# Fourth layer's attention: natural scores ahead of the next queries, and values and gate products ahead of the turned maxima

## The reference, cut to what matters

```python
x = x + tanh(g_xattn[3]) * L3_xattn(layernorm(x), ctx, Wq, bq, Wk, bk, Wv, bv, Wp, bp)
# L3_xattn, 16 heads of 8 features:
q = (x @ Wq.T + bq).reshape(Bx, Nx, H, D)
k = (ctx @ Wk.T + bk).reshape(Bx, -1, H, D)
v = (ctx @ Wv.T + bv).reshape(Bx, -1, H, D)
att = softmax(einsum('bnhd,bthd->bhnt', q, k) / sqrt(D))
y = einsum('bhnt,bthd->bnhd', att, v).reshape(Bx, Nx, C) @ Wp.T + bp
# followed by x = x + tanh(g_ffn[3]) * L3_ffn(layernorm(x), ...), a mixture of 8 experts, 2 per token
```

## Time and profile before

| what | us |
|---|---|
| median of 3 runs | 1149.16 (1143.81 to 1149.33) |
| span of the profiled execution, first to last instruction | 1134.3 |
| median less that span | 14.9 |
| a pass of the fourth layer's attention, plain (pass 10) | 9.04 |
| the same, pass 9 | 10.96 |

### The profile page before, as it was taken

How to read it: one execution, slowest core, us unless ns; L and a number is a source line. 1 busy time by engine, 2 the same in 40 slices (tenths; PEclk the granted TensorE clock), 3 DMA queues, 4 the chain that set the end, 5 groups by cost and what they waited for, 6 DMA issues and landing times.

```text
span 1134.3 us, 17733 instructions
## 1 busy us (share of the span) xinstructions
PE 1006.4 (89%) x6226; PEld 611.8 (54%) x6226; DVE 740.0 (65%) x2216; ACT 496.2 (44%) x980; POOL 427.0 (38%) x659
## 2 busy tenths in 40 slices
PE   9999999998899979998999999999988882899970
PEld 6356666665444454357855666665444441466650
DVE  2747999997866677757676555556876766433334
ACT  2656566763344455532243333323543430454524
POOL 0062444444544252034234220004256637166651
PEclk7999999998999978998699999999998985899985
DMA  8078000000000030000044433330000001501116
GB/s 197 1 271 233 1 1 1 1 2 19 1 1 2 2 119 1 0 1 1 1 109 98 90 83 76 76 76 1 1 23 30 27 25 48 202 28 35 34 37 233
DMA packets 38712, 62.01 MB, mean 55 GB/s; under 512 B 6145, under 2 KB 22248, under 8 KB 37858
## 3 DMA queue, kind: packets, MB, share of 16 engines
q1 hardware_dynamic: 34018, 52.40, 17.0%
q0 software_dynamic: 4608, 8.50, 2.3%
HBM read 40.47 MB, written 21.45 MB: 55 GB/s over the span
## 4 chain that ended last, share of the span: by engine, by line
PE 54%; issue 24%; DVE 12%; ACT 3%; DMA 3%; POOL 1%; another core or an unknown queue 1%; SPq 0%; POOLq 0%; DVEq 0%
PE bank L1196 6%; PE bank L484 5%; PE bank L527 5%; PE bank L1212 4%; PE bank L1258 3%; PE bank L630 3%; PE bank L428 3%; PE bank L513 2%; PE bank L1269 2%; PE bank L520 2%; ACT att L1477 1%; DMA big_a<-gates 1%; PE bank L700 1%; PE bank L649 1%
## 5 line engine op out<-in xcount | busy, mean ns | idle before, releaser
L1196 PE MATMUL bank<-big_b 128*128 128x512 f32 x288 | 135.8, 596 | 0.0
L2280 DVE TENSOR_REDUCE nmax<-bank 128x16 f32<-128x1024 f32 x64 | 78.0, 1219 | 55.4 <-PE bank L636 29.7
L2029 POOL DMA_INDIRECT expert_outs<-big_a,big_b x80 | 77.9, 974 | 68.0 <-DVE big_a L2915 44.1
L1682 ACT ACTIVATE att<-bank 128x512 f32<-128x512 f32 (+1 forms) x72 | 43.0, 597 | 134.7 <-PE bank L1196 132.3
L1807 POOL TENSOR_SCALAR xn<-xw,mean,rstd 128x128 f32<-128x128 f32 x62 | 49.8, 811 | 125.7 <-DVEq L2841 90.2
L1212 PEld LDWEIGHTS bank<-big_b,att 128*128 128x128 f32 (+1 forms) x576 | 72.9, 191 | 32.0 <-issue 19.1
L2020 POOL DMA_INDIRECT expert_rows<-xw,big_b x64 | 63.4, 990 | 67.2 <-DVEq L2382 50.5
L2777 DVE TENSOR_TENSOR att<-att,bank 128x512 f32<-128x512 f32 (+1 forms) x72 | 49.3, 684 | 56.6 <-PE bank L1212 53.6
L1477 ACT ACTIVATE att<-bank 128x1024 f32<-128x1024 f32 x64 | 62.0, 1021 | 43.8 <-PE bank L676 43.8
L1212 PE MATMUL bank<-big_b,att 128*128 128x128 f32 (+1 forms) x576 | 77.9, 278 | 3.7 <-DVE xw L2137 2.4
L1258 PE MATMUL bank<-big_b 128*128 128x384 f32 (+2 forms) x192 | 73.1, 523 | 0.7 <-ACT big_b L1709 0.7
(11 more groups left out here) (443 smaller groups left out, 2179.6 us busy)
## 6 DMA issues: line engine op xcount, KB each, us to landing
big_a<-gates SPq DMA_DIRECT2D x14, 1024.0 KB, 10.2
expert_rows<-big_b SPq DMA_DIRECT2D x1, 5240.0 KB, 19.4
expert_outs<-big_b SPq DMA_DIRECT2D x1, 4096.0 KB, 31.7
big_a<-expert_outs SPq DMA_DIRECT2D x16, 256.0 KB, 5.4
big_a<-expert_rows SPq DMA_DIRECT2D x1, 2620.0 KB, 15.3
big_a<-in_mask SPq DMA_DIRECT2D x2, 1024.0 KB, 12.0
big_b<-in_w_in SPq DMA_DIRECT2D x1, 2048.0 KB, 8.8
out<-xw SPq DMA_DIRECT2D x8, 256.0 KB, 3.9
```

Source lines behind the costliest of these rows:

```text
L1196: mm = nc.tensor.matmul(bank[2 * (n % 3) + k][:, :], w13[:, k, c * 128:(c + 1) * 128], xnT_all[:, g * GW:(g + 1) * GW], start=True, stop=True)
L2029: nc.gpsimd.indirect_dma_start(outs3, bass.IndirectOffsetOnAxis(numbers3[:, ex, i:i + 1].bitcast(u32), 0), xs[:, ex, i, 0:D], None, bounds ...
L2280: nc.vector.tensor_reduce(nmax[:, j], psum[:, 2048:3072].rearrange("p (h t) -> p h t", t=T), AX.X, MAX, negate=True).then_inc(s.free, 1)
```

## The change

In each pass PE issues the second tile's natural scores ahead of the next queries, and the values and gate products ahead of the turned maxima. The waits inside the helpers stay as they are.

```diff
                         weighted(b)
+                        if b + 1 < B:
+                            natural(b + 1, 1)
                         if b + 2 < B:
                             queries(b + 2)
-                        if b + 1 < B:
-                            natural(b + 1, 1)
                         if b:
                             output_features(b - 1)
                         if b + 1 < B:
                             turned(b + 1)
+                            values(b + 1)
                             maxima_transposes(b + 1)
-                            values(b + 1)
                         if b:
                             projected(b - 1)
```

## The result

The changed kernel takes 1157.22 us in the median (1152.3 to 1165.74, 7 runs), the kernel before 1149.16 (1143.81 to 1151.71, 7 runs). The ratio is 1.0117, interval [1.0081, 1.0152]: slower by 1.2%, some 13.4 us. (The ratio is the recorded estimate with its interval; the two medians alone are 8.1 us apart, 1.0070.) Forecast was 1148 and no change, range 1140 to 1157.

A forecast was written before the change was run, and what follows sets the result against it. Each attention pass was taken as a ring through TensorE and ScalarE's exponentials, TensorE nearly the bound. +8.8, -8.5, -0.4 and -1.3 made -1.4 us; with 0 for truly late passes, -1 was taken: 1149.2 to 1148 us, range 1140 to 1157.

The forecast's parts named there:

- The wait before L716: TensorE, before `output_features`: waiting for the queries' evacuation adds 0.68 us in each of passes 1 to 13, +8.8 in all.
- the ring: Each attention pass: weighted, TensorE's middle part, shift, ScalarE's exponentials, weighted again; time added between weighted and shift lengthens it.
- L664's wait gone, shift at 6.53, plain pass 9.06: TensorE, plain pass: `maxima_transposes` loses its 0.40 us wait, shift comes at 6.53 instead of 6.25, pass 9.06 against 9.04.
- The smaller unknown: Earlier `natural` on TensorE may wait for the first tile's reduction, up to 0.27 us in five passes; 0 to 1.4, taken 0.
- The sum, -1.4 us: Attention stage: +8.8 new wait, -8.5 L664's waits, -0.4 pass 14, -1.3 waits for `y`, 0 pass 0.
- L664's waits in passes 1 to 12, 7.4, and in pass 13, 1.1: -8.5: TensorE's idle before `maxima_transposes`, waiting for the split maxima, was to vanish, saving 8.5 us.
- the bound put on the late odd passes: Passes 7, 9, 11: if TensorE is truly behind at L716, less idle is saved; sum 0, -1 taken, -3 to +3 kept.
- The end of a matmul: TensorE instruction ends are computed, not observed, so late releases are true times and the sum would be 0, not -1.4.
- B: Late odd passes 7, 9, 11 and 13 mend, faster: up to 10 us go, 1139, or half, 1144; chance 0.21.
- C: The wait for the queries' evacuation is not given back, slower: 13 x 0.68 = 8.8 us, 1158; chance 0.12.
- D: TensorE's clock: the new 0.68 us gap brings 5 more low-clock stretches, costing 8.5 us, 1157; chance 0.07.

The follow-up runs named there:

- the longer evacuation: Changed kernel with ScalarE copying the queries a second time, into an unused buffer, ahead of the true evacuation; 1166.38 us, one run.
- turned between: Kernel before with both swaps and `output_features` moved behind `turned`; ratios to the kernel before 0.9959, 0.9955 and 0.9942.
- the slots earlier: Both swaps with `turned` ahead of `output_features`, plus VectorE's slots of even passes ahead of the second reduction; ratio to the kernel before 1.0013.
- after_again: Changed kernel run again with unchanged code, beside the kernel before on a second-kind chip; ratio 1.0114 to the kernel before.
- before_again: Kernel before run again with unchanged code and profiled a second time, on a second-kind chip; 1138.92 us.

## Why the prediction was wrong, point by point

**The wait before L716**, predicted 0.68 in 13 passes: measured 0.66 in 13 where no release is held, and in the first profile of the changed kernel 0.66 in nine and 1.2 to 5.3 in the other four. Right in itself, and that the ring pays for it is shown by the longer evacuation (0.36 more wait, 0.35 more pass).

**L664's wait gone, shift at 6.53, plain pass 9.06**: L664 without a wait, 6.50, 9.03. Right. But by the prediction's own rows 9.06 is 0.28 more, not less, than the 8.78 of a pass that does not wait for `y`; the forecast saving rests on the long waits of L664 in the late odd passes, and on those for `y`.

**The smaller unknown, taken as 0**: in even passes from 4 on `natural` starts at 1.17 and not 1.00, and they take 9.20 us and not 9.06. It costs 0.17 in five passes, 0.8 us, inside its bounds of 0 to 1.4.

**The sum, -1.4 us**: the step "L664's waits in passes 1 to 12, 7.4, and in pass 13, 1.1: -8.5" was mis-sized. With the sends out of the way L664's wait is 0.33 in odd passes and 0.40 in even ones, about 4.8 us in all; the other 3.7 were held releases that happened to be charged to this step. With 4.8 for the 8.5, and the 0.8 above, the sum is +3.1. Undisturbed, the change costs 0.25 us a pass: 2.5 us over passes 1 to 10, about 3 over 13. That agrees with the 1.0038 [1.0001, 1.0075] of the first kind of chip.

**The step that failed** is the bound put on the late odd passes: "the sum is -1.4 + 1.4 = 0 [...] keep -3 to +3 for this case". It took the late releases as a fixed property of those passes, which the change could at most uncover. The windows with the sends late show that they need POOL's sends; the profile of before had POOL's L2020 in every long pass, and I did not lay the two engines side by side. By the semaphore records between 790 and 950 us, 30 to 46 of TensorE's releases come more than 0.3 us after their modelled ends in each profile of the second kind with the sends in place, up to 6.1 us, and none in the six profiles of the first kind, where the largest is 0.04. No release of ScalarE or VectorE is late in any of them, though on the second kind some of their records are missing. Pass 13 of the changed kernel shows it, in the order of time on POOL, ScalarE and TensorE:

```profile
927.59 1.08 POOL L2020 DMA_INDIRECT expert_rows<-xw,big_b  x1 [8.61 <-DVEq L2382]
...
936.61 0.98 POOL L2020 DMA_INDIRECT expert_rows<-xw,big_b  x1 [0.30 <-issue]
```

```profile
936.23 0.59 ACT L1482 COPY att<-bank 128x512 f32<-128x512 f32 x1 [5.63 <-remote]
937.72 0.47 ACT L1463 ACTIVATE vals<-bank,colb 128x256 f32<-128x256 f32 x1 [0.90 <-remote]
```

```profile
938.34 0.66 PE L716 MATMUL bank<-ident,y 128*128 128x128 f32 x2 [5.27 <-ACT vals L1463]
```

Eight sends run from 927.6 to 937.6. `weighted` is issued at 930.32 and lasts 1.07, but ScalarE starts the copy of its output only at 936.23; the queries' evacuation is behind that copy in ScalarE's order, and L716, with all of TensorE's queue, behind the evacuation. The trace's semaphore records agree: the releases of `weighted`, `natural` and `queries` come at 936.21, 937.66 and 937.70, so the evacuation waits for the last of them. With the changed order such a delay lands on TensorE in full: L716 waits 15.3 us where 8.6 was the undisturbed sum, and in pass 9 the exponentials, 0.45 behind the shift in a plain pass, follow it by 3.17 (890.86 to 894.03) with the end of it charged to the next `weighted`.

That `natural` covered the same delay in the order of before is not shown, because there the delay falls elsewhere. In its pass 13 the releases of `weighted` and `queries` come 0.34 and 0.43 us after their modelled ends, and the longest hold, 3.74, is that of L664. The same eight sends start 2.1 us ahead of that pass's `weighted` (909.53 and 911.63) and not 2.7:

```profile
909.53 1.07 POOL L2020 DMA_INDIRECT expert_rows<-xw,big_b  x1 [5.20 <-DVEq L2382]
```

Between 790 and 950 us the longest hold is 2.5 to 3.8 us in the three profiles of before, the second swap alone and turned between, 4.9 with the slots earlier, and 5.2 to 6.1 in the four in which L716 follows the queries at once. So the new order moves the sends against TensorE's steps as well as opening a wait, and the runs do not separate the two.

**The end of a matmul.** The Trainium skill (Perfetto Trace Analysis, Per-engine timelines) has it that a TensorE instruction's end is computed. The runs agree: the late releases were the true times, by which the stage must be read. But no version of that rule bounds how late a release may be, and I used it as if it did.

**The rivals.** B did not happen: the odd passes mend only with the sends gone or on the other kind of chip. C had the right size, 1158, by luck and for the wrong reason: L664's wait was given back. D happened in part: in the changed kernel pass 10 ran at 0.50 and pass 13 at 0.67, where before had 1.00 and 0.73; the first kind of chip shows 1.00 in all 13 passes of every profile. Pass 10 follows the halt of pass 9, so I read the low clock as its consequence; that was argued, not isolated. As time the parts are known: busy 8.8 and idle 6.6 us more in the first pair of profiles, 5.7 and 9.6 in the second (`after_again` and `before_again`). Which causes which stays open. Open too: why the first swap alone costs more than both (1.0189 and 1.0114 on different chips of one kind, with equal waits at L716; by medians alone 1.0150 and 1.0120), and what in the chip holds the releases.

## What to carry to other kernels

Before a step is moved ahead of another, look for what the step that moves was covering: here `natural` hid an evacuation of 1.31 us, and the next step on the same queue needed it. When two adjacent swaps are good in part, put the covering work where the latency now is: the same two swaps with `turned` moved in between give 0.994 to 0.996 of the kernel before on both kinds of chips. A release that comes late without a reason on its own engine should be laid beside every other engine's row at that time, DMA issues included, before it is priced; and such a delay must be priced at each place where the new order leaves a wait open.

## What the runs showed of the hardware

On one kind of chip (kernel before at 1146 to 1149 us) TensorE's semaphore releases are held around the time at which POOL issues indirect transfers to memory, by up to 6.1 us with four or eight of them in a row, and are let go in a bunch: 936.21, 937.66 and 937.70 for steps started at 930.32, 931.32 and 932.38. With 32 of them in a row a release was held for 30.8 us, and that pass takes 43.6 us in place of 9.0. On the other kind (1112 to 1116 us) the same program with the same sends shows none of it, no release over 0.04 us late and 9.2 us a pass. The change's ratio was 1.0117 and 1.0114 in two comparisons on the one kind, and 1.0038 on the other, from the same code.
